# Second chunk's row scatters one stage later, two GpSimd scalings at other places of the stage

## What is computed

```python
x = x + attn(layernorm(x))          # then
x = x + ffn(layernorm(x))

# attn: q, k, v = short convolution (4 taps) of x @ qkv_w ; beta, alpha: gates per token and head
def step(S, inp):                   # one token; S: [heads, 128, 128]
    S = S * alpha_t
    kv = einsum('bhk,bhkv->bhv', k_t, S)
    S = S + einsum('bhk,bhv->bhkv', k_t, (v_t - kv) * beta_t)
    o_t = einsum('bhk,bhkv->bhv', q_t, S)
# o is normalised, gated with z * sigmoid(z), projected with out_w

# ffn: logits = x @ W_router + b_router; two best experts per token
y = relu(x @ W1[e] + b1[e]) @ W2[e] + b2[e]      # only for the tokens of expert e
```

## Time and profile before

| | before |
|---|---|
| median of 3 runs | 1396.27 us (1392.47 to 1402.48) |
| the profiled execution | 1399.73 us |
| its span, first to last instruction | 1397.9 us |
| PE / DVE / POOL busy | 1199.9 / 1164.4 / 707.9 us |
| mean granted TensorE clock | 0.965 |

### The profile page before, as it was taken

One profiled execution on the slowest core, in us unless ns is written; L12 is line 12 of the kernel. 1 busy time (PEld: TensorE's weight loads), 2 busy tenths in 40 slices (PEclk: granted clock), 3 DMA queues, 4 the chain that ended last, 5 costly groups with the idle time before them and its releaser, 6 DMA issues.

```text
span 1397.9 us, 34191 instructions
## 1 busy us (share of the span) xinstructions
PE 1199.9 (86%) x12203; PEld 944.0 (68%) x12203; DVE 1164.4 (83%) x2531; ACT 832.0 (60%) x2536; POOL 707.9 (51%) x598
## 2 busy tenths in 40 slices
PE   0355999999999999999999999999999989479991
PEld 0233868686868687777777777777777767358881
DVE  6878898989898998989898989897989783578875
ACT  1252666666666666657566666756566655358884
POOL 3151727464555656473828292928192822235552
PEclk9997999999999999999999999999999998789996
DMA  6031212222221222131313141313121223432225
GB/s 208 0 98 32 73 35 73 47 69 62 54 63 53 62 54 64 52 68 48 84 34 91 28 98 25 103 28 88 30 85 43 73 55 98 104 96 78 76 65 181
DMA packets 163176, 97.10 MB, mean 69 GB/s; under 512 B 115623, under 2 KB 148269, under 8 KB 161988
## 3 DMA queue, kind: packets, MB, share of 16 engines
q1 hardware_dynamic: 124932, 82.25, 21.6%
q10 hardware_dynamic: 33536, 4.20, 2.1%
q0 software_dynamic: 4544, 8.47, 1.9%
HBM read 73.31 MB, written 24.61 MB: 70 GB/s over the span
## 4 chain that ended last, share of the span: by engine, by line
DVE 37%; PE 21%; POOL 17%; issue 10%; DMA 9%; SPq 3%; ACT 3%; POOLq 0%; DVEq 0%; ACTq 0%
DVE blkT L1060 9%; POOL kq L637 9%; DVE Y_sb L1056 9%; DMA blkN<-scr_n 4%; PE kx L1553 3%; POOL decay L629 3%; POOL rows_in L609 2%; DVE Gs L1204 2%; POOL kq L620 2%; DMA scr_n<-area 2%; PE rc L1717 2%; SPq L477 2%; DVE blkN L1047 1%; DVE area L1170 1%; DVE Y_sb L1043 1%
## 5 line engine op out<-in xcount | busy, mean ns | idle before, releaser
L637 POOL TENSOR_TENSOR kq<-tapA,area 128x256 f32<-128x256 f32 x256 | 252.0, 998 | 93.6 <-DVE area L1146 92.8
L758 ACT ACTIVATE area<-pj,taps 128x256 f32<-128x256 f32 x256 | 123.1, 481 | 142.7 <-PE pj L1567 136.5
L1056 DVE TENSOR_TENSOR Y_sb<-blkT,blkN 128x4 f32<-128x4 f32 (+18 forms) x304 | 169.5, 558 | 10.5
L609 POOL DMA_INDIRECT rows_in<-rowbuf,dest x64 | 64.6, 1009 | 202.1 <-DVE dest L1132 175.2
L1143 DVE SCALAR_TENSOR_TENSOR tapA<-pj,taps,tapA 128x256 f32<-128x256 f32 x256 | 122.2, 477 | 53.4 <-ACT tapA L758 51.6
L1553 PE MATMUL kx<-kq 128*128 128x128 f32 x1024 | 141.0, 285 | 20.0 <-ACT area L767 9.6
L1553 PEld LDWEIGHTS kx<-kq 128*128 128x128 f32 x1024 | 128.7, 197 | 38.4 <-issue 21.8
L620 POOL TENSOR_TENSOR kq<-kq,area 128x1024 f32<-128x1024 f32 x64 | 151.1, 2362 | 0.0
L1060 DVE TENSOR_REDUCE blkT<-Y_sb 128x2 f32<-128x4 f32 (+18 forms) x304 | 142.4, 469 | 5.2
L758 ACT ACTIVATE tapA<-pj,taps 128x256 f32<-128x256 f32 x256 | 123.0, 480 | 0.0
L1146 DVE SCALAR_TENSOR_TENSOR area<-pj,taps,area 128x256 f32<-128x256 f32 x256 | 121.4, 474 | 0.0
(11 more groups left out here) (307 smaller groups left out, 3613.2 us busy)
## 6 DMA issues: line engine op xcount, KB each, us to landing
area<-scr_alpha SPq DMA_DIRECT2D x32, 512.0 KB, 4.2
area<-scr_acum SPq DMA_DIRECT2D x32, 512.0 KB, 4.0
blkN<-scr_n SPq DMA_DIRECT2D x32, 256.0 KB, 4.4
area<-rows_in SPq DMA_DIRECT2D x39, 130.0 KB, 2.3
scr_n<-area SPq DMA_DIRECT2D x128, 32.0 KB, 1.6
area<-rows_out SPq DMA_DIRECT2D x4, 1024.0 KB, 8.1
rows_in<-rows_in SPq DMA_DIRECT2D x8, 260.0 KB, 3.8
kq<-in_x SPq DMA_DIRECT2D x4, 512.0 KB, 6.2
```

Source lines behind the costliest of these rows:

```text
L637: nc.gpsimd.tensor_tensor(dst[:, n % H, :], tapA[:, n % RING, :], tapB[:, n % RING, :], ALU.add).then_inc(conv_done, 1)
L758: ins = nc.scalar.activation(dst[:, n % RING, :], pj[n % 2][:, k:k + GT], ACT.Copy, scale=taps[:, t, k:k + 1])
L1056: ins = nc.vector.tensor_tensor(p4, bc(blkT[:, r0:, j:].rearrange("p r (o m) -> p r o m", o=1), [128, nr, w, wd]), bc(blkN[:, j:j + w, j:] ...
```

## The change

1. The 4 scatters of `sc` become 2 there (chunk 0) and 2 (chunk 1) that are issued in the next stage at the place of `last.15`, before that addition. The last of the deferred pairs are issued after the last stage, and behind the final route.
2. `ka.0` stands ahead of `last.0`, not behind it.
3. `sp.1` stands ahead of `last.13`, `last.14` and `last.15`, not only ahead of `last.15`.

POOL's words are now: diag.0, ka.0, last.0 to last.3, diag.1, last.4 to last.7, sp.0, aq.0, last.8, last.9, aq.1, last.10, last.11, ka.1, last.12, sp.1, last.13, last.14, two scatters of the group before, last.15, nr, sc with two scatters. The other engines' orders are the same. The list of words is wrapped anew; in it only the two words move.

```diff
@@ ORDER @@
-            proj.0 proj.1 taps.0 taps.1 diag.0 first.0 v.0.0 proj.2 m.1.0 taps.2 al.0 first.1 proj.3 m.0.0 last.0 taps.3
-            rdiag.0 me.1.0 v.0.1 first.2 proj.4 first.3 ka.0 last.1 me.0.0 m.1.1 taps.4 proj.5 me.1.1 ks.0.0 m.0.1 taps.5
+            proj.0 proj.1 taps.0 taps.1 diag.0 first.0 v.0.0 proj.2 m.1.0 taps.2 al.0 first.1 proj.3 m.0.0 ka.0 last.0
+            taps.3 rdiag.0 me.1.0 v.0.1 first.2 proj.4 first.3 last.1 me.0.0 m.1.1 taps.4 proj.5 me.1.1 ks.0.0 m.0.1
...
-            first.14 inv.0 taps.15 ks.1.1 last.13 rhs.1.0 inv.1 inv.2 last.14 inv.3 inv.4 first.15 rhs.1.1 u.1.0 inv.5
-            kq.0.0 u.1.1 ue.1.0 g.0.1 inv.6 ue.1.1 o.1.0 o.1.1 ktr.0.1 sq.1.0 inv.7 s2 ac.1 sd.1.0 sp.1 sq.1.1 kd.0.1 inv.8
...
+            sm v.1.1 scale.0 bi ks.1.0 kd.0.0 first.14 inv.0 taps.15 ks.1.1 sp.1 last.13 rhs.1.0 inv.1 inv.2 last.14
...
@@ route(), step "sc" @@
                     pool.sem_inc(sends, 1)
-                    for c in range(GC):
-                        for k in range(2):
-                            nc.gpsimd.indirect_dma_start(
-                                rows_in, bass.IndirectOffsetOnAxis(ap=dest[:, k, c:c + 1], axis=0), rowbuf[:, c, k, :], None,
-                                bounds_check=SPARE - 1, oob_is_err=False).then_inc(scattered, 16)
+                    send(0)
+
+            def send(c):
+                for k in range(2):
+                    nc.gpsimd.indirect_dma_start(
+                        rows_in, bass.IndirectOffsetOnAxis(ap=dest[:, k, c:c + 1], axis=0), rowbuf[:, c, k, :], None,
+                        bounds_check=SPARE - 1, oob_is_err=False).then_inc(scattered, 16)
@@ stages() @@
                         route(step, r, par)
+                        if (step, *arg) == ("last", NT - 1) and r > 0:
+                            send(1)
```

More of the change, by code:

```diff
@@ L249, in preln_delta_moe_kernel @@
         ORDER = """
-            proj.0 proj.1 taps.0 taps.1 diag.0 first.0 v.0.0 proj.2 m.1.0 taps.2 al.0 first.1 proj.3 m.0.0 last.0 taps.3
-            rdiag.0 me.1.0 v.0.1 first.2 proj.4 first.3 ka.0 last.1 me.0.0 m.1.1 taps.4 proj.5 me.1.1 ks.0.0 m.0.1 taps.5
-            scan.0 first.4 m.1.2 proj.6 me.0.1 rdiag.1 ks.0.1 last.2 last.3 first.5 me.1.2 proj.7 m.0.2 m.1.3 al.1 taps.6
-            diag.1 first.6 taps.7 last.4 proj.8 first.7 kk.0.0 me.0.2 me.1.3 m.0.3 last.5 proj.9 last.6 xl.0 rhs.0.0 me.0.3
@@ L264, in preln_delta_moe_kernel @@
-            st.1.1 xs.1 tj sc
+            proj.0 proj.1 taps.0 taps.1 diag.0 first.0 v.0.0 proj.2 m.1.0 taps.2 al.0 first.1 proj.3 m.0.0 ka.0 last.0
+            taps.3 rdiag.0 me.1.0 v.0.1 first.2 proj.4 first.3 last.1 me.0.0 m.1.1 taps.4 proj.5 me.1.1 ks.0.0 m.0.1
+            taps.5 scan.0 first.4 m.1.2 proj.6 me.0.1 rdiag.1 ks.0.1 last.2 last.3 first.5 me.1.2 proj.7 m.0.2 m.1.3
+            al.1 taps.6 diag.1 first.6 taps.7 last.4 proj.8 first.7 kk.0.0 me.0.2 me.1.3 m.0.3 last.5 proj.9 last.6
@@ new lines, in preln_delta_moe_kernel @@
+            xl.0 rhs.0.0 me.0.3 last.7 sp.0 scan.1 nm.0.0 taps.8 kk.0.1 u.0.0 taps.9 aq.0 nm.0.1 kk.1.0 first.8 last.8
+            nm.1.0 kk.1.1 nm.1.1 proj.10 ue.0.0 rhs.0.1 taps.10 o.0.0 first.9 proj.11 first.10 proj.12 u.0.1 taps.11
+            first.11 taps.12 last.9 sd.0.0 proj.13 ktr.0.0 ue.0.1 first.12 xl.1 aq.1 last.10 no.0 no.1 sq.0.0 proj.14
+            taps.13 last.11 st.0.0 ac.0 sd.0.1 taps.14 g.0.0 o.0.1 first.13 ka.1 st.0.1 sq.0.1 proj.15 last.12 v.1.0
+            sm v.1.1 scale.0 bi ks.1.0 kd.0.0 first.14 inv.0 taps.15 ks.1.1 sp.1 last.13 rhs.1.0 inv.1 inv.2 last.14
@@ new lines, in preln_delta_moe_kernel @@
+            inv.3 inv.4 first.15 rhs.1.1 u.1.0 inv.5 kq.0.0 u.1.1 ue.1.0 g.0.1 inv.6 ue.1.1 o.1.0 o.1.1 ktr.0.1 sq.1.0
+            inv.7 s2 ac.1 sd.1.0 sq.1.1 kd.0.1 inv.8 scale.1 inv.9 inv.10 at.0.0 inv.11 ktr.1.0 inv.12 g.1.0 last.15
+            kd.1.0 inv.13 rms.0 inv.14 sd.1.1 ktr.1.1 kd.1.1 rms.1 gn.0.0 kq.0.1 gn.0.1 gt.0.0 inv.15 at.0.1 z.0.0
+            inv.16 gt.0.1 gte.0.0 nr g.1.1 xt inv.17 gte.0.1 z.0.1 zt.0.0 xe lg out.0 gn.1.0 zt.0.1 inv.18 rk gn.1.1
+            gt.1.0 inv.19 gt.1.1 x2.0 inv.20 gte.1.0 inv.21 kq.1.0 gte.1.1 pf out.1 zg.0.0 z.1.0 tp zt.1.0 zg.0.1 ps
@@ L265, in preln_delta_moe_kernel @@
+            st.1.0 z.1.1 zt.1.1 zg.1.0 zg.1.1 xs.0 x2.1 to at.1.0 kq.1.1 at.1.1 ti st.1.1 xs.1 tj sc
             """
```

## The result

| | before | after |
|---|---|---|
| median, 20 runs each on one chip | 1394.35 us (1390.97 to 1403.85) | 1400.22 us (1395.51 to 1406.82) |
| profiled execution | 1399.73 us | 1396.62 us |
| ratio of the times | | 1.0031, 95% interval 1.0017 to 1.0045 |

The changed kernel is 0.3% slower, where I had forecast 0.6% faster; that is within the 1% that I had called no difference, and 1.2 us above the top of my range.

What follows compares the result with a forecast made beforehand. No engine alone was taken as the bound: DVE, PE and POOL share the chain. Head 6.6, edit 3 0 and new place 2.0 us sum to 8.6 us, median 1396.27 to 1387.7 us; range 1378 to 1399.

Steps and rivals of the forecast that it cites:

- The read of T: Head: with two of four scatters gone, PE's wait for the inverse's DMA falls by 40%, 3.0 us gained in 13 stages.
- The head's cap: Head: POOL's gain is capped by PE's path, 23.14 to 22.86 us a stage, 3.6 us gained in 13 stages.
- a gain of 6.6: Head, edit 1: sum of the cap's 3.6 us and the DMA wait's 3.0 us.
- The scan waits for at most one addition: Head, edit 2: POOL reaches ka.0 before DVE reaches scan.0, so the scan waits at most 0.7 us, not 1.56 us.
- Edit 2 at nothing: Head: ka.0 ahead of last.0 adds no work and stays early enough for ScalarE's ring; its gain is within the 6.6 us.
- Edit 3 at nothing: Start of the inverse: sp.1 earlier loses 0.2 us in 8 stages, gains about 0.35 us in 5, nothing in sum.
- the 1.8 us of my bound: Start of the inverse, edit 3: the most it could win; the most it could lose was 2.6 us.
- The new place: Inverse: last.15, later behind the moved scatters, holds a different DVE product, 0.15 us gained a stage, 2.0 us in all.
- The scatter's hold: Inverse: the moved scatters' effect on DVE, costed at nothing because L1344 stays at 674 to 693 ns beside indirect DMAs.
- the rival's mechanism: Inverse: rival that scatters hold DVE, two issues of 1.0 us a stage, 26 us in 13 stages, 1415.7 us; chance 0.07.
- the head is hidden anyway: Head: rival that the read lands late as before, kk stays at 23.1 us, gain 0 to 3.6 us, 1394 to 1398; chance 0.18.

Runs made afterwards that it cites:

- h1: Changed kernel with the two scatters left at a stage's head issued behind ka.0, after the read of T: ratio 0.9962 to the kernel before.
- f1: The changed kernel itself, unaltered, run and profiled a second time: ratio 1.0021 to the kernel before.
- f4: Kernel before with only one wait added, POOL's last.2 waiting for scan.0: ratio 0.9989 to the kernel before.
- e3: Kernel before with only sp.1 moved ahead of last.13 and last.14: 1396.52 us, ratio 0.9999 to the kernel before.
- h2: The changed kernel itself, unaltered, run beside h3 on one chip: 1420.06 us, ratio 1.0015 to the kernel before.
- h3: Changed kernel with POOL's last.2 waiting for scan.0: 1416.30 us, ratio 0.9991 to the kernel before.
- i2: Repeat of g4, the changed kernel with all four scatters ahead of last.15 and ka.0 at its old place: ratio 0.9843 to the kernel before.
- h4: Kernel before with only all four scatters moved ahead of last.15, ka.0 and sp.1 at their old places: ratio 0.9867 to the kernel before.
- g4: Changed kernel with all four scatters ahead of last.15 and ka.0 back at its old place: ratio 0.9855 to the kernel before.
- e1: Kernel before with only the scatters' move (edit 1), ka.0 and sp.1 not moved: 1404.5 us, ratio 1.0043 to the kernel before.
- e2: Kernel before with only ka.0 moved ahead of last.0 (edit 2): 1417.65 us, ratio 1.0145 to the kernel before.

## Why the prediction was wrong

- **The read of T (40% off its wait, 3.0 us): this step failed.** I had argued that two of the four scatters leave the time of the read. But the pair that leaves wasn't in it: it was issued 1.6 and 2.8 us after the read, and its packets moved when T had landed in 10 of 13 stages. With two scatters the first matmul comes as late as with four (7.62 to 8.18 against 7.73 to 7.94 us in the mean); with none beside the read it comes at 7.08 to 7.20 us. h1 shows that it is their time that does it. SyncE's issue of the read and the queue's packets were in the trace of before, and I didn't put them beside the earlier trace rows. How a scatter makes the read late isn't shown: in f1's stage with the latest first matmul (9.34 us) the last packet of the two scatters started at 7.05 us. Without this term 5.6 us of gain were still forecast; the sign turned with the next three steps.
- **The head's cap (3.6 us).** The mechanism was right: POOL's path got shorter and PE's path now sets kk.0.1, 15.25 us after the first matmul. What I left out is that the old head had slack. Before, kk.0.1 stood at 23.14 us as long as the first matmul came by 7.88 us, so most waits for T cost nothing. Now every one is paid. I took a mean wait, and its jitter has a second price, the clock (last section). With all terms the head lost 3.5 us where I had forecast a gain of 6.6: from the write to kk.0.1 it takes 23.52 us in the mean of before, f4 and e3 and 23.79 in that of after, f1 and h2.
- **"The scan waits for at most one addition": wrong.** It had held in every stage of before, because one long instruction ran when the scan came. Behind it I assumed that a waiting engine gets its turn after one instruction. In after and h2 the scan waited for the rest of a run of four additions and for diag.1, up to 3.0 us, in 3 and 4 of 13 stages (in f1 in 1), 0.9 to 1.5 us each at kk.0.1. With the wait 4 us of the loss went away (h3 against h2).
- **Edit 2 at nothing: wrong.** Alone it costs 1.45% through the ring, a path that I checked only for the three edits together. Together with edit 1 a small cost stays: with all scatters late, ka.0 ahead takes 1377.44 and ka.0 in its old place 1374.89 us (intervals overlap), and both have the same 13 stages (857.2 and 857.7 us). The difference lies ahead of them: in 11 profiles with ka.0 ahead the first like stage begins at 264.4 to 267.7 us, mean 265.7, and in 9 with ka.0 in its old place at 261.7 to 265.6, mean 262.8. That fits the missing 3 us of the medians. No run has edits 1 and 3 without edit 2, so for the changed kernel itself this is argued from where the like stages begin. The cause stays open: 1.0 us of it is between the first two writes (68.3 against 67.3 us), the rest ahead of the first write, where ka.0 isn't issued at all.
- **Edit 3 at nothing: not told from it by the medians** (0.9999 alone; with all scatters late 1396.92 us in i2 against 1399.31 in h4, which has sp.1 in its old place, intervals overlap). My timing was wrong: in a regular stage the first product ends no later than before, 4.56 us after the start of L1038, and where it had ended up to 0.75 us later it no longer does. In before's 13 stages that is some 3 us, more than the 1.8 us of my bound, and the like stages of i2 and g4 (856.9 and 857.7 us) are 4 to 5 us shorter than h4's (862.0).
- **The new place (2.0 us won): right in sign, sized too high.** From the end of the first product to the next write took 26.73 us before. It takes 26.51 us where the 64-element product is free (0.22 us) and 26.83 where the second scatter holds it (0.85 us). The scatter's hold, which I had costed at nothing by L1344, is there, in 9, 6 and 2 of 13 stages, at 0.3 us each: the rival's mechanism at a tenth of its price. In sum the three profiles stand at 347.6, 346.7 and 345.5 us against 347.5.

The rival that came nearest is "the head is hidden anyway", by its place and by its reason (the read lands late as before), but its time, 1394 to 1398, was also below what was measured: it had no lost turn and no cost of edit 2. In the mean of three profiles each the 13 stages take 879.4 us with two scatters at the head and 878.6 with four, and with ka.0 ahead they begin 2.9 us later. Together that is close to the measured 4 to 6 us. But it can't prove the shares: the 13 stages of the changed kernel range over 17 us from one execution to the next.

## What to carry to other kernels

Before moving work away from a transfer, write in one column when the transfer is issued and lands and when each piece of that work moves its own data. Here a scatter moved its packets 1.5 us and more after its issue, so the pair issued 1.6 and 2.8 us behind the read moved them mostly when the read was over. The wrong half was moved; moving the other half too turned +0.3% into -1.3%. A path made shorter exposes the jitter of the next one, which a covered path hid, so the new limit is to be priced with its spread and not with its mean. And a dependent long instruction should not meet a run of short ones of the engine it excludes: where it arrives decided between 2.3 and 5.6 us here.

## What the runs showed of the hardware

**A waiting VectorE instruction can lose several turns in a row.** The scan (two SBUF inputs) lost to the rest of a run of additions and to a longer instruction behind them, up to 3.3 us (5.62 us for 2.28 in e1). The Trainium skill ("SBUF — State Buffer", section "Who interferes with whom") has one of the two blocked for the other's length; the trace agrees for each instruction, but the length that counts is that of the run. In other stages the scan went in between the additions (4.85 us for four, the good stage above). By arrival: in e1 it lost at 10.39 to 10.87 us after the write and won from 11.03 us on, though twice also at 10.62 and 10.68 us.

**A scatter sometimes holds a VectorE product and sometimes not**, at the same distance. After, two stages, DVE and then POOL (the second of two scatters):

```profile
512.03 0.85 DVE L1062 TENSOR_TENSOR Y_sb<-blkT,blkN 128x64 f32<-128x64 f32 x1
...
644.76 0.22 DVE L1062 TENSOR_TENSOR Y_sb<-blkT,blkN 128x64 f32<-128x64 f32 x1
```

```profile
511.73 0.97 POOL L611 DMA_INDIRECT rows_in<-rowbuf,dest  x1 [0.30 <-issue]
...
644.46 0.97 POOL L611 DMA_INDIRECT rows_in<-rowbuf,dest  x1 [0.30 <-issue]
```

With four scatters in a row there the same product took 0.22 or 0.23 us in all stages of seven profiles. I have no rule for it.

**A wait of TensorE for T is often followed by a stretch at half clock.** f1, PE's first matmul of a stage, and the stretches ahead of it and behind it (length, busy time and count by engine, then PEclk, DMA share and GB/s; 1.00 is 2.4 GHz, 0.50 is 1.2 GHz):

```profile
818.84 0.18 PE L1386 MATMUL kx<-wab_hi 128*16 128x16 f16 x1 [2.14 <-DMA T<-scr_t]
```

```profile
816.00:819.00 3.00, 0.82 (x7) 0.35 (x8) 1.10 (x4) 0.84 (x2) 3.00 (x3) 1.00 0.77 155
819.20:826.00 6.80, 6.80 (x75) 3.42 (x70) 4.98 (x7) 2.35 (x6) 5.04 (x5) 0.50 0.12 28
```

The stretches seen here were 3.4 or 6.8 us long. A single one makes kk.0.1 some 1.6 us later (16.86 instead of 15.25 us behind the first matmul in h3's stage at 664.58 us), a double one 3.1 us. Over eleven profiles with two or four scatters at the head (all but e2), 143 stages: no stretch in 69 stages whose first matmul came under 7.8 us after the write, 3 in 28 between 7.8 and 8.1 us, 23 in 46 from 8.1 us on. In the eight profiles without scatters beside the read there was none in 104 stages, 103 of them under 7.8 us. e2 has its stretches behind another pause, the 1.7 us for ScalarE shown above. So where T came late enough to leave TensorE idle for a microsecond or two, half of the stages paid for it a second time. That the wait brings the half clock, and not the scatters beside it, isn't shown: no profile has a long wait for T without them. Whether the changed kernel has more such stages than before, three profiles each can't say (1, 7 and 1 against 2, 2 and 1 in before, f4 and e3).
